# Fusion block on one core: q and k rows regrouped by one transfer of 128 partitions, weight columns in dimension-major order

## The chip, the core and the metric

The kernel runs on one core of a Trainium2 chip. Its engines are TensorE (PE, matmuls; PEld is its loading of weights), VectorE (DVE), ScalarE (ACT), GpSimd (POOL) and SyncE (SP). SyncE computes nothing here; it issues DMA transfers from a queue, in the order of the program. The metric is the time of the whole program on the device, in microseconds (us), as the median of several runs. Lower is better.

## What is computed

The reference makes a sequence `h` of 128 rows out of a state-space kernel and 77 rows of text, for each of 32 images (205 rows of 1024 numbers), and sends it through attention and a linear layer:

```python
h = _L0_tok_ref(log_dt, Lambda, x, 1024)
h = jnp.concatenate([h, txt], axis=1)                       # (32, 205, 1024)
h = h + attn(_layernorm(h), wq, wk, wv, wo)
h = h + ffn(_layernorm(h), W_base, b_base, enc0, enc1, ...)

# attn: NH = 32 query heads, NKV = 8 key and value heads, HD = 32
q = (x @ wq).reshape(b, s, NH, HD)
k = (x @ wk).reshape(b, s, NKV, HD)
v = (x @ wv).reshape(b, s, NKV, HD)
k, v = jnp.repeat(k, 4, axis=2), jnp.repeat(v, 4, axis=2)
scores = jnp.einsum('bihd,bjhd->bhij', q, k) * HD ** -0.5   # causal mask
out = jnp.einsum('bhij,bjhd->bihd', softmax(scores), v)
return out.reshape(b, s, NH * HD) @ wo
```

## The kernel before

The program has three parts, one after the other. `ssm` makes the 128 rows of each image and ends near 185 us. `attention` is a software pipeline over the 32 images, which are called blocks. `tail` multiplies by `wo` and runs the linear layer, from about 1797 us to the end.

In `attention` each engine runs the same `step(b)` for b from -4 to 32. In a step, TensorE works on several blocks at once. It projects block b+2: units `q` 0 to 7, `k` 0 and 1, `v` 0 and 1, each of 24 matmuls. It takes the scores of block b+1 a first time, for their maxima (`score_rows`, L1000 to L1007). And it takes the transposed scores of block b (`scores`, L956 and L959), whose exponentials ScalarE and GpSimd turn into weights for `weigh` (L986). In the first steps only some of that exists: step -2 projects block 0, step -1 projects block 1 and takes the maxima of block 0, step 0 is the first with everything.

All numbers are carried as a high and a low half-precision part. A `q` unit gives 128 columns of the projection, which are four heads of 32 dimensions, so that `qsh` and `qsl` hold in partition 32r + d the dimension d of head 4n + r. The scores want something else: `qst` holds for each head 96 partitions, high, high and low part of its 32 dimensions (`kst`: high, low, high), so that one matmul makes all three products, and two rows more, 96 and 97, with the maxima (`mh`, `ml`). Bringing q and k from the one layout into the other is `restack` (L572). Since it changes partitions, it is done by DMA: for each of the three parts and each r of four, 32 partitions are copied to 32 others. A k unit holds four of the eight key heads, which are moved in the same way. Blocks take turns in two buffers, `qst0`/`qst1` and `kst0`/`kst1`.

SyncE's order in a step is:

1. K1, Q1: the restacks of the second half of the heads of block b+1, whose last unit was projected at the end of the step before;
2. `shift_rows(1)`: two rows of maxima for block b (heads 16 to 31), L617 and L618;
3. in step -1 alone: the loads `ahead` (L597), `wo` with 4 MB and 14 smaller ones, that the tail wants;
4. the four transposes of block b+3 (L623, L624), twice a high and a low part, which TensorE projects in the next step. ScalarE may only overwrite the source `xfh` when they have landed (`high_part`, L717);
5. K0, Q0: the restacks of the first half of block b+2;
6. `shift_rows(0)`: the rows of maxima for heads 0 to 15 of block b+1.

K0 or K1 waits for the low part of its `k` unit and until the scores of an older block no longer need the buffer (`st_filled`); Q0 waits for `q` unit 3 and Q1 for `q` unit 7 (`pj_lo`, counted up by VectorE at L868). TensorE waits for Q and K at L990 and L991 in front of L1000, and for the rows of maxima in front of L956.

Of the kernel before, what the change touches and what calls it, by code (L numbers as in the profile page):

```python
# [8 lines left out]
F16 = mybir.dt.float16  # L9
BF16 = mybir.dt.bfloat16  # L10
I32 = mybir.dt.int32
ALU = mybir.AluOpType
# [4 lines left out]
P = 128  # L17
# [4 lines left out]
D = 1024  # L22
TXT = 77
S = H + TXT
# [397 lines left out]
def attention(nc, ahead, hcat, acat, st, qkv, arena, all_peaks, peaks_in, ksc, spare):  # L422
# [7 lines left out]
    with ExitStack() as ctx:  # L430
# [13 lines left out]
        qsh, qsl = sb("qsh", [P, KC, S], F16), sb("qsl", [P, KC, S], F16)  # L444
        ksh, ksl = sb("ksh", [P, 2, S], F16), sb("ksl", [P, 2, S], F16)
        mh, ml = sb("mh", [NH // 2, 2, S], F16), sb("ml", [NH // 2, 2, S], F16)
        qst = [sb(f"qst{i}", [STACK + 2, NH, S], F16) for i in range(2)]
        kst = [sb(f"kst{i}", [STACK + 2, NKV, S], F16) for i in range(2)]
        vh = [sb(f"vh{i}", [P, 2, NKV, HD + 1], F16) for i in range(3)]
        vl = [sb(f"vl{i}", [P, 2, NKV, HD + 1], F16) for i in range(3)]  # L450
# [1 line left out]
        p32 = arena[:, 0:12 * S].rearrange("p (a k x) -> p a k x", a=2, k=3)  # L452
        ph = sb("ph", [P, 2, 3, 2 * S], F16)
        pl = sb("pl", [P, 2, 3, 2 * S], F16)
        mx = sb("mx", [P, 2, NH])
        seen = sb("seen", [P, REP, P], BF16)
        rden = sb("rden", [P, 2, REP])
        ao = arena[:, 12 * S:12 * S + 2 * D].rearrange("p (h t x) -> p h t x", h=2, t=2)
# [93 lines left out]
        def free_place(eng, kind, n, b):  # L552

            if kind == "q":
                wait(eng, q_in[n // 4], 16 * 12 * (b + 2))
            if kind == "k":
                wait(eng, k_in[n], 16 * 12 * (b + 2))
            if kind == "v":
                wait(eng, av_done, 8 * b)
            if kind == "m":  # L560
                wait(eng, m_in[n], 32 * (b + 1 - n))
# [3 lines left out]
        @block.sync  # L565
        def _(sp):
            def restack(parts_, dst, cs, arrived):

                for k, src in enumerate(parts_):
                    rows = dst[k * HD:(k + 1) * HD].rearrange("d (c r) i -> d c r i", r=4)  # L570
                    for r in range(4):
                        sp.dma_start(rows[:, cs, r, :], src[r * HD:(r + 1) * HD, cs, :]).then_inc(arrived, 16)  # L572

            Q_PARTS, K_PARTS = (qsh, qsh, qsl), (ksh, ksl, ksh)
            HALVES = (slice(0, KC // 2), slice(KC // 2, KC))

            def step(b, par, has):
                base = before(b, par)
                rows = units(has)
                nxt = 1 - par  # L580
                if has["max"]:

                    wait(sp, st_filled, 24 * b)
                    prev = parts(b - 1)
                    wait(sp, pj_lo, before(b - 1, nxt) + at(units(prev), "k", 1) + 1)
                    restack(K_PARTS, kst[nxt], slice(1, 2), k_in[1])
                    wait(sp, pj_lo, before(b - 1, nxt) + at(units(prev), "q", NKV - 1) + 1)
                    restack(Q_PARTS, qst[nxt], HALVES[1], q_in[1])
                if has["att"]:

                    wait(sp, pj_lo, base + at(rows, "m", 1) + 1)
                    shift_rows(1, par)
                if b == -1:

                    sp.wait_ge(w_lo, 2 * KC)
                    for dst, src, arrived in ahead:
                        sp.dma_start(dst, src).then_inc(arrived, 16)  # L597
                if has["turn"]:

                    wait(sp, pj_filled, base)  # L600
                    turn(0, nxt, b + 3)
                    turn(1, nxt, b + 3)
                if has["qkv"]:

                    wait(sp, pj_lo, base + at(rows, "k", 0) + 1)
                    wait(sp, st_filled, 24 * b + 12)
                    restack(K_PARTS, kst[par], slice(0, 1), k_in[0])
                    wait(sp, pj_lo, base + at(rows, "q", 3) + 1)
                    restack(Q_PARTS, qst[par], HALVES[0], q_in[0])
                if has["max"]:  # L610

                    wait(sp, pj_lo, base + at(rows, "m", 0) + 1)
                    shift_rows(0, nxt)

            def shift_rows(half, to):
                heads = slice(half * (NH // 2), (half + 1) * (NH // 2))
                sp.dma_start(qst[to][STACK:STACK + 1, heads, :], mh[:, half, :]).then_inc(m_in[half], 16)  # L617
                sp.dma_start(qst[to][STACK + 1:STACK + 2, heads, :], ml[:, half, :]).then_inc(m_in[half], 16)  # L618

            def turn(t, to, n):  # L620
                r, cols = ((P, slice(0, P)), (TROWS, slice(P, P + TROWS)))[t]
                sp.wait_ge(x_lo, 4 * n + 2 * t + 2)
                sp.dma_start_transpose(out=xth[:, to, :, cols], in_=xfh[0:r, t, :]).then_inc(xt_in[t], 16)  # L623
                sp.dma_start_transpose(out=xtl[:, to, :, cols], in_=xfl[0:r, t, :]).then_inc(xt_in[t], 16)  # L624

            steps(sp, step)
            for q in a_out:
                sp.wait_ge(q, 32 * B)
# [152 lines left out]
        def _(dve):  # L781
# [58 lines left out]
            def take_maxes(b, j, base, ks, late_read):  # L840
                for k in ks:
                    dve.wait_ge(s_filled, 24 * (b + 1) + 3 * j + k + 1)
                    if j == 0 and k == 0:

                        wait(dve, pj_filled, base)
                    if j == NKV // 2 and k == 0 and late_read:

                        dve.wait_ge(pj_filled, base + late_read)
                    src = psS[(j + k) % 2]
                    if k == 0:  # L850
                        if j == 0:
                            dve.wait_ge(mask_ok, 1)
                        for r in range(REP):
                            m = dve.tensor_tensor_reduce(seen[:, r, :], src[:, r * P:(r + 1) * P], mask[:, 0, :], 1.0, LEAST,  # L854
                                                         ALU.add, ALU.max, mx[:, 0, 4 * j + r:4 * j + r + 1])
                        m.then_inc(s_read, 1)
                    else:
                        v = src[0:TXT, 0:2 * S].rearrange("p (h i) -> p h i", i=S)
                        dst = mx[0:TXT, 1, 4 * j + 2 * k - 2:4 * j + 2 * k]
                        dve.tensor_reduce(dst, v, AX.X, ALU.max).then_inc(s_read, 1)  # L860

            def split_unit(b, par, bank, kind, m, count_):
# [81 lines left out]
        def _(pe):  # L944
            pe.wait_ge(const_ok, 1)

            def scores(b, par, g, k):

                if g % 4 == 0 and k == 0:

                    pe.wait_ge(m_in[g // 4], 32 * (b + 1))
                K, Q = kst[par], qst[par]
                wait(pe, exp_done, 24 * b + 3 * g + k - 1)
                ps = psT[(g + k) % 2]
                if k < 2:
                    m = pe.matmul(ps[:, 0:2 * S], K[:, g, 0:P], Q[:, 4 * g + 2 * k:4 * g + 2 * k + 2, :],  # L956
                                  start=True, stop=True)
                else:
                    m = pe.matmul(ps[0:TXT, 0:REP * TXT], K[:, g, P:S], Q[:, 4 * g:4 * g + 4, P:S],  # L959
                                  start=True, stop=True)  # L960
                m.then_inc(st_filled, 1)

# [27 lines left out]
            def score_rows(b, par, j, k):  # L990


                pe.wait_ge(q_in[j // 4], 16 * 12 * (b + 1))
                pe.wait_ge(k_in[j // 4], 16 * 12 * (b + 1))
                K, Q = kst[par], qst[par]
                wait(pe, s_read, 24 * b + 3 * j + k - 1)
                ps = psS[(j + k) % 2]
                if k == 0:
                    for r in range(REP):
                        m = pe.matmul(ps[:, r * P:(r + 1) * P], Q[0:STACK, 4 * j + r, 0:P], K[0:STACK, j, 0:P],  # L1000
                                      start=True, stop=True)
                else:
                    v = ps[0:TXT, 0:2 * S].rearrange("p (h i) -> p h i", i=S)
                    pe.matmul(v[:, :, P:S], ident_bf[0:TXT, 0:TXT], mask[0:TXT, 0:2, 0:TXT],
                              start=True, stop=False, skip_group_check=True)
                    for r in range(2):
                        m = pe.matmul(v[:, r, :], Q[0:STACK, 4 * j + 2 * (k - 1) + r, P:S], K[0:STACK, j, :],  # L1007
                                      start=False, stop=r == 1, skip_group_check=True)
                m.then_inc(s_filled, 1)

            def unit(kind, n, bank, b, par, ks):
# [16 lines left out]
                elif not last:  # L1028
                    return
                elif kind == "m":  # L1030

                    heads = slice(n * (NH // 2), (n + 1) * (NH // 2))
                    pe.wait_ge(s_read, 24 * (b + 1) + 12 * (1 - n))
                    pe.transpose(ps[0:NH // 2, 0:P], mx[:, 0, heads], ident[:])
                    m = pe.transpose(ps[0:NH // 2, P:S], mx[0:TXT, 1, heads], ident[0:TXT, 0:TXT])
                if last:
                    m.then_inc(pj_filled, 1)

# [439 lines left out]
```

## Time and profile before

| | us |
|---|---|
| median of 3 runs | 2941.69 |
| lowest and highest | 2940.85, 2944.85 |
| the profiled execution | 2947.19 |
| its span, first to last instruction | 2945.1 |
| TensorE busy | 2695.8 |
| VectorE busy | 1940.4 |
| ScalarE busy | 1201.6 |
| GpSimd busy | 1144.2 |

The mean granted clock of TensorE in the profiled execution was 0.969 of full. All times of the trace count from the start of the span. In a list of waits a row is "who at which line <- whom it waited for", with total, number and longest. In a timeline, "SPq L572 ... x4" are four issues by SyncE's queue, with the time from the start of the first to the end of the last; a value in brackets at the end is how long the engine had been idle, and for whom. The releaser is the one that the profile shows as the last. Windows sum the busy time of each engine within a stretch; a granted clock of 0.50 is 1.2 GHz and one of 1.00 is 2.4 GHz.

### The profile page before, as it was taken

To read this page: it belongs to the slowest core of one execution; us is meant where nothing else is said; L and a number is where in the kernel's file an instruction comes from. 1 tells how busy PE (TensorE), PEld (TensorE's weight loads), DVE (VectorE), ACT (ScalarE), POOL (GpSimd) and SP (SyncE) were. 2 spreads that over 40 slices of the span, in tenths; PEclk is the share of its full clock that TensorE was granted. 3 is DMA by queue.
4 is the path that set the end of the run, shared out by engine and by line. 5 is a ranking of instruction groups with operands and counts; after the bars stand their busy time and mean duration, and the time that the engine had idled before them with its cause. 6 is when DMAs were issued, how large, how long until landed. Compare 5 with 4: busy or idle time off the path is not lost. (4 is left out here: it accounts for less than half of the span.)

```text
span 2945.1 us, 70977 instructions
## 1 busy us (share of the span) xinstructions
PE 2695.8 (92%) x27456; PEld 1949.7 (66%) x27456; DVE 1940.4 (66%) x5569; ACT 1201.6 (41%) x2506; POOL 1144.2 (39%) x1811
## 2 busy tenths in 40 slices
PE   1948699999999999999999986999999999999999
PEld 1837589989898998989899972444444444444444
DVE  8964488887888888788888774744444444444443
ACT  4342466676766767666666663101010100101010
POOL 2751266565656656566565563101111010101110
PEclk9978899999999999999999995899999999999999
DMA  7754534434343443435344325354554555454543
GB/s 240 190 123 112 87 88 96 98 77 98 82 102 85 93 98 77 99 82 103 81 95 87 66 55 178 79 139 115 136 123 128 131 119 134 119 140 115 136 122 81
DMA packets 564334, 324.72 MB, mean 110 GB/s; under 512 B 501016, under 2 KB 519704, under 8 KB 563520
## 3 DMA queue, kind: packets, MB, share of 16 engines
q1 hardware_dynamic: 541488, 256.35, 39.2%
q10 hardware_dynamic: 22512, 63.84, 6.9%
q8 instruction: 219, 3.59, 0.5%
q14 instruction: 115, 0.94, 0.1%
HBM read 116.49 MB, written 80.61 MB: 67 GB/s over the span
## 5 line engine op out<-in xcount | busy, mean ns | idle before, releaser
L1018 PE MATMUL psJ<-xth,qh 128*128 128x205 f16 x2048 | 520.3, 254 | 52.4 <-DMA xtl<-xfl 46.9
L689 POOL TENSOR_TENSOR pl<-arena,ph 128x410 f16<-128x410 f32 (+1 forms) x512 | 499.5, 995 | 94.7 <-ACT ph L765 94.7
L1020 PE MATMUL psJ<-xth,ql 128*128 128x205 f16 x2048 | 519.0, 253 | 0.0
L1019 PE MATMUL psJ<-xtl,qh 128*128 128x205 f16 x2048 | 518.6, 253 | 0.0
L684 POOL TENSOR_SCALAR_AFFINE_SELECT arena<-arena 128x256 f32<-128x256 f32 (+1 forms) x768 | 331.6, 438 | 475.5 <-ACT arena L758 454.5
L1243 POOL TENSOR_TENSOR arena<-stage,arena 128x1024 f32<-128x1024 f32 x52 | 122.2, 2349 | 938.1 <-DVE stage L1286 938.1
L1257 ACT CAST xh<-arena 128x1024 f16<-128x1024 f32 x52 | 54.3, 1045 | 998.3 <-DVE arena L1295 998.3
L758 ACT ACTIVATE arena<-psT,escale 128x410 f32<-128x410 f32 (+1 forms) x768 | 401.1, 567 | 119.0 <-PE psT L959 59.7
L765 ACT CAST ph<-arena 128x410 f16<-128x410 f32 (+1 forms) x768 | 334.8, 500 | 15.8 <-POOL arena L684 15.5
L1286 DVE SCALAR_TENSOR_TENSOR stage<-ps5O,osc,h_in 128x512 f32<-128x512 f32 x104 | 78.0, 751 | 390.6 <-PE ps5O L1383 390.6
L860 DVE TENSOR_REDUCE mx<-psS 77x2 f32<-77x410 f32 x512 | 295.4, 577 | 39.8 <-PE psS L1007 32.3
L1381 PE MATMUL ps5F<-wfh,xth 128*128 128x512 f16 x832 | 315.4, 379 | 3.1 <-DMA xtl<-xl 2.0
L1382 PE MATMUL ps5O<-wol,ath 128*128 128x512 f16 x832 | 316.3, 380 | 0.0
L1381 PE MATMUL ps5O<-woh,ath 128*128 128x512 f16 x832 | 316.3, 380 | 0.0
L1383 PE MATMUL ps5O<-woh,atl 128*128 128x512 f16 x832 | 316.2, 380 | 0.0
L854 DVE CUSTOM_DVE_ANT_0 seen<-psS,mask 128x128 bf16<-128x128 f32 x1024 | 235.3, 286 | 121.5 <-PE psS L1000 121.5
L1382 PE MATMUL ps5F<-wfl,xth 128*128 128x512 f16 x832 | 315.3, 379 | 0.0
L1383 PE MATMUL ps5F<-wfh,xtl 128*128 128x512 f16 x832 | 315.3, 379 | 0.0
L986 PE MATMUL psO<-vh,ph 128*128 128x33 f16 (+1 forms) x3072 | 261.2, 178 | 5.1 <-issue 4.7
L986 PE MATMUL psO<-vl,ph 128*128 128x33 f16 (+1 forms) x3072 | 260.4, 178 | 0.0
L986 PE MATMUL psO<-vh,pl 128*128 128x33 f16 (+1 forms) x3072 | 260.4, 178 | 0.0
L986 PEld LDWEIGHTS psO<-vh,ph 128*128 128x128 f16 (+1 forms) x3072 | 245.2, 97 | 7.3 <-issue 6.3
(234 smaller groups left out, 6143.7 us busy)
## 6 DMA issues: line engine op xcount, KB each, us to landing
a_in<-acat SPq DMA_DIRECT2D x52, 512.0 KB, 3.8
h_in<-hcat SPq DMA_DIRECT2D x52, 512.0 KB, 4.6
qst<-qsh SPq DMA_DIRECT2D x512, 51.2 KB, 2.1
out<-stage SPq DMA_DIRECT2D x51, 512.0 KB, 3.1
hcat<-ob SPq DMA_DIRECT2D x64, 256.0 KB, 4.5
xin<-hcat ACTq DMA_DIRECT2D x32, 512.0 KB
acat<-arena ACTq DMA_DIRECT2D x64, 256.0 KB
qst<-qsl SPq DMA_DIRECT2D x256, 51.2 KB, 2.5
```

The lines of the kernel that those rows point to most:

```text
L684: pool.affine_select(out=v, in_=v, compare_op=ALU.is_ge, fill=0.0, base=0, pattern=[[0, v.shape[1]], [1, w]], channel_multiplier=-1).then_ ...
L689: pool.tensor_tensor(view(pl, g % 2, k), view(p32, g % 2, k), view(ph, g % 2, k), ALU.subtract).then_inc(lo_pool, 1)
L758: act.activation(view(p32, g % 2, k), ps_view(psT[(g + k) % 2], k), ACT.Exp, scale=(escale[:, 0:1] if k < 2 else escale[0:TXT, 0:1])).then ...
L765: act.copy(view(ph, g % 2, k), view(p32, g % 2, k)).then_inc(hi_done, 1)
L860: dve.tensor_reduce(dst, v, AX.X, ALU.max).then_inc(s_read, 1)
L986: m = pe.matmul(o[:, t, r, :], p, v[0:T[j], j, g, :], start=n == 0, stop=n == len(list_) - 1)
L1018: pe.matmul(ps[:, 0:S], wh[:, k, c], xth[:, par, k, 0:S], start=k == 0, stop=False)
L1019: pe.matmul(ps[:, 0:S], wh[:, k, c], xtl[:, par, k, 0:S], start=False, stop=False)
L1020: m = pe.matmul(ps[:, 0:S], wl[:, k, c], xth[:, par, k, 0:S], start=False, stop=k == KC - 1)
L1381: pe.matmul(ps[h][:], th[:, k, :], wh[:, k, c], start=k == 0, stop=False)
L1382: pe.matmul(ps[h][:], th[:, k, :], wl[:, k, c], start=False, stop=False)
L1383: m = pe.matmul(ps[h][:], tl[:, k, :], wh[:, k, c], start=False, stop=k == KC - 1)
```

## The change

The columns of `wq` and `wk` are put in another order before they go to the device: within each group of 128, dimension first and head second, where it was head first. So `qsh` now holds in partition 4d + r the dimension d of head 4n + r. Read in order of partitions, that is the order (d, r), and the destination `qst` is laid out to match: its heads are stored by half, r and chunk, `[STACK + 2, 2, REP, NKV // 2, S]` instead of `[STACK + 2, NH, S]`. One transfer then reads 128 partitions with 4 x 205 neighbouring numbers each (1640 bytes) and writes 32 partitions with four such runs. For k it is 128 partitions with 205 numbers each. A restack has 3 issues instead of 12, and the semaphores are counted in 16 x 3 instead of 16 x 12. `mx`, the maxima, is stored in the same order as `qst`, and the matmuls address q and the maxima accordingly: L956 takes its two heads from two places 820 numbers apart, where they were neighbours. Products, sums and their number are the same.

```diff
-        qst = [sb(f"qst{i}", [STACK + 2, NH, S], F16) for i in range(2)]
+        qst = [sb(f"qst{i}", [STACK + 2, 2, REP, NKV // 2, S], F16) for i in range(2)]
-        mx = sb("mx", [P, 2, NH])
+        mx = sb("mx", [P, 2, 2, REP, NKV // 2])
...
-                wait(eng, q_in[n // 4], 16 * 12 * (b + 2))
+                wait(eng, q_in[n // 4], 16 * 3 * (b + 2))
...
                 for k, src in enumerate(parts_):
-                    rows = dst[k * HD:(k + 1) * HD].rearrange("d (c r) i -> d c r i", r=4)
-                    for r in range(4):
-                        sp.dma_start(rows[:, cs, r, :], src[r * HD:(r + 1) * HD, cs, :]).then_inc(arrived, 16)
+                    sp.dma_start(dst[k * HD:(k + 1) * HD], src[:, cs, :]).then_inc(arrived, 16)
...
-                    restack(Q_PARTS, qst[nxt], HALVES[1], q_in[1])
+                    restack(Q_PARTS, qst[nxt][:, 1], HALVES[1], q_in[1])
...
-                sp.dma_start(qst[to][STACK:STACK + 1, heads, :], mh[:, half, :]).then_inc(m_in[half], 16)
+                sp.dma_start(qst[to][STACK:STACK + 1, half], mh[:, half, :]).then_inc(m_in[half], 16)
...
-                        dst = mx[0:TXT, 1, 4 * j + 2 * k - 2:4 * j + 2 * k]
+                        dst = mx[0:TXT, 1, j // 4, 2 * k - 2:2 * k, j % 4]
...
-                    m = pe.matmul(ps[:, 0:2 * S], K[:, g, 0:P], Q[:, 4 * g + 2 * k:4 * g + 2 * k + 2, :],
+                    m = pe.matmul(ps[:, 0:2 * S], K[:, g, 0:P], Q[:, g // 4, 2 * k:2 * k + 2, g % 4, :],
...
+        if name in ("L0_attn_wq", "L0_attn_wk"):
+            a = a.reshape(D, -1, 4, HD).transpose(0, 1, 3, 2).reshape(D, -1)
```

The order of the instructions on TensorE, VectorE, ScalarE and GpSimd is as before. SyncE's queue is shorter in two places that matter below. The first is in step -1, K1 and Q1 of block 0 and behind them the first of the loads `ahead`. Before:

```order
L572 DMA kst0<-ksh 32x205 x4
L572 DMA kst0<-ksl 32x205 x4
L572 DMA kst0<-ksh 32x205 x4
L572 DMA qst0<-qsh 32x4x205 x8
L572 DMA qst0<-qsl 32x4x205 x4
L597 DMA stage<-in_L0_attn_wo 128x8x1024
```

Now:

```order
L573 DMA kst0<-ksh 32x4x205
L573 DMA kst0<-ksl 32x4x205
L573 DMA kst0<-ksh 32x4x205
L573 DMA qst0<-qsh 32x4x820 x2
L573 DMA qst0<-qsl 32x4x820
L598 DMA stage<-in_L0_attn_wo 128x8x1024
```

24 issues stand in front of the load of `wo` before, six now. In a row of the queue the numbers behind the names are the shape of the destination.

The second place is later in the same step, between the last two transposes of block 2 and the rows of maxima of block 0 (`mh`, `ml`), with K0 and Q0 of block 1 between them. Before:

```order
L624 DMA_TRANSPOSE xtl<-xfl 128x8x80
L572 DMA kst1<-ksh 32x205 x4
L572 DMA kst1<-ksl 32x205 x4
L572 DMA kst1<-ksh 32x205 x4
L572 DMA qst1<-qsh 32x4x205 x8
L572 DMA qst1<-qsl 32x4x205 x4
L617 DMA qst0<-mh 1x16x205
L618 DMA qst0<-ml 1x16x205
```

Now:

```order
L624 DMA_TRANSPOSE xtl<-xfl 128x8x80
L573 DMA kst1<-ksh 32x4x205
L573 DMA kst1<-ksl 32x4x205
L573 DMA kst1<-ksh 32x4x205
L573 DMA qst1<-qsh 32x4x820 x2
L573 DMA qst1<-qsl 32x4x820
L617 DMA qst0<-mh 1x16x205
L618 DMA qst0<-ml 1x16x205
```

Here too 24 issues between the transposes and `mh` have become six. The same pattern stands twice in each later step.

## Rows read from the trace of the kernel before

**Rows 1.** Windows: busy us (x instructions) by engine, granted clock, DMA share, GB/s.

```profile
800.00:1000.00 200.00, 192.49 (x2923) 179.68 (x2924) 163.05 (x553) 129.45 (x294) 119.48 (x220) 1.00 0.42 89
```

**Rows 2.** Waits of TensorE, 600 to 1600 us: total us, times, longest us.

```profile
PE psS L1004 <- DVE mx L854: 30.9, 44, 1.1
```

**Rows 3.** Waits of SyncE's DMA queue, 600 to 1600 us.

```profile
SPq L572 <- PE psT L959: 37.2, 22, 2.7
```

**Rows 4.** Waits of TensorE over the whole span.

```profile
PE psJ L1018 <- DMA xtl<-xfl: 46.9, 1, 46.9
...
PE psS L1000 <- DMA qst<-qsl: 5.9, 1, 5.9
```

**Rows 5.** Timeline of ScalarE and TensorE: start us, us, work, [idle before <-releaser].

```profile
310.62 0.72 ACT L717 ACTIVATE xin<-xin,nmean 128x512 f32<-128x512 f32 x1 [17.17 <-DMA xtl<-xfl]
...
313.35 0.32 PE L1004 MATMUL psS<-mask,ident_bf 77*77 77x154 bf16 x1 [14.03 <-DVE mx L860]
...
329.69 0.86 PE L956 MATMUL psT<-qst,kst 98*128 98x410 f16 x2 [12.09 <-DMA qst<-ml]
```

**Rows 6.** Timeline of SyncE's queue, 247 to 330 us: start us, us, issues.

```profile
248.33 2.52 SPq L572 DMA_DIRECT2D kst<-ksh  x4
...
280.74 0.59 SPq L597 DMA_DIRECT2D stage<-in_L_attn_wo  x1
...
282.88 11.87 SPq L597 DMA_DIRECT2D mk<-in_L_ffn_mask  x1
...
305.80 1.28 SPq L623 DMA_TRANSPOSE xth<-xfh  x1
...
311.16 2.49 SPq L572 DMA_DIRECT2D kst<-ksh  x4
...
327.74 0.59 SPq L618 DMA_DIRECT2D qst<-ml  x1
```

**Rows 7.** Tile qst, 600 to 1600 us: duration ns min/median/max, then us to landing.

```profile
L956 PE MATMUL psT<-qst,kst x341: 333/337/340, 599.8 to 1593.1; 98*128 98x410 f16 x171
L572 SPq DMA_DIRECT2D qst<-qsh x340: 585/602/1832, 599.7 to 1600.0; - x170
...
L959 PE MATMUL psT<-qst,kst x171: 298/299/328, 602.5 to 1594.8; 98*77 98x308 f16 x171
...
DMA to landing us min/median/max: 1.9/2.1/4.0
```

**Rows 8.** Timeline of VectorE, 255 to 300 us.

```profile
260.64 0.37 DVE L868 TENSOR_TENSOR qsl<-psJ,qsh 128x205 f16<-128x205 f32 x1
...
294.89 0.35 DVE L866 SCALAR_TENSOR_TENSOR ml<-psJ,mh 16x205 f16<-16x205 f32 x1
```

**Rows 9.** Windows, as in rows 1, in the order of time.

```profile
266.00:272.00 6.00, 5.87 (x36) 5.25 (x37) 2.66 (x11) 0.15 (x1) 0.00 (x0) 0.50 0.10 23
285.00:299.00 14.00, 13.82 (x165) 13.55 (x163) 9.13 (x47) 1.55 (x5) 2.53 (x13) 1.00 1.05 327
330.00:333.00 3.00, 3.00 (x20) 2.56 (x19) 1.42 (x9) 2.38 (x3) 0.65 (x2) 0.50 0.09 22
...
1748.00:1753.00 5.00, 4.61 (x58) 3.52 (x57) 3.13 (x13) 3.68 (x9) 3.26 (x5) 0.50 0.02 5
```

**Rows 10.** Timelines of SyncE's queue, VectorE and TensorE, 1727 to 1748 us.

```profile
1727.78 2.43 SPq L572 DMA_DIRECT2D kst<-ksh  x4
...
1745.58 0.59 SPq L618 DMA_DIRECT2D qst<-ml  x1
...
1735.43 0.35 DVE L866 SCALAR_TENSOR_TENSOR ml<-psJ,mh 16x205 f16<-16x205 f32 x1
...
1747.54 0.86 PE L956 MATMUL psT<-qst,kst 98*128 98x410 f16 x2 [4.74 <-DMA qst<-ml]
```

**Rows 11.** Timelines of SyncE's queue and TensorE, a step in the middle.

```profile
1024.97 0.59 SPq L618 DMA_DIRECT2D qst<-ml  x1
...
1030.03 0.51 PE L956 MATMUL psT<-qst,kst 98*128 98x410 f16 x2
```

More of the change, by code:

```diff
@@ L554, in free_place @@
             if kind == "q":
-                wait(eng, q_in[n // 4], 16 * 12 * (b + 2))
+                wait(eng, q_in[n // 4], 16 * 3 * (b + 2))
             if kind == "k":
-                wait(eng, k_in[n], 16 * 12 * (b + 2))
+                wait(eng, k_in[n], 16 * 3 * (b + 2))
             if kind == "v":
@@ L585, in step @@
                     wait(sp, pj_lo, before(b - 1, nxt) + at(units(prev), "k", 1) + 1)
-                    restack(K_PARTS, kst[nxt], slice(1, 2), k_in[1])
+                    restack(K_PARTS, kst[nxt][:, 4:8], slice(1, 2), k_in[1])
                     wait(sp, pj_lo, before(b - 1, nxt) + at(units(prev), "q", NKV - 1) + 1)
-                    restack(Q_PARTS, qst[nxt], HALVES[1], q_in[1])
+                    restack(Q_PARTS, qst[nxt][:, 1], HALVES[1], q_in[1])
                 if has["att"]:
@@ L606, in step @@
                     wait(sp, st_filled, 24 * b + 12)
-                    restack(K_PARTS, kst[par], slice(0, 1), k_in[0])
+                    restack(K_PARTS, kst[par][:, 0:4], slice(0, 1), k_in[0])
                     wait(sp, pj_lo, base + at(rows, "q", 3) + 1)
-                    restack(Q_PARTS, qst[par], HALVES[0], q_in[0])
+                    restack(Q_PARTS, qst[par][:, 0], HALVES[0], q_in[0])
                 if has["max"]:
@@ L615, in shift_rows @@
             def shift_rows(half, to):
-                heads = slice(half * (NH // 2), (half + 1) * (NH // 2))
-                sp.dma_start(qst[to][STACK:STACK + 1, heads, :], mh[:, half, :]).then_inc(m_in[half], 16)
-                sp.dma_start(qst[to][STACK + 1:STACK + 2, heads, :], ml[:, half, :]).then_inc(m_in[half], 16)
+                sp.dma_start(qst[to][STACK:STACK + 1, half], mh[:, half, :]).then_inc(m_in[half], 16)
+                sp.dma_start(qst[to][STACK + 1:STACK + 2, half], ml[:, half, :]).then_inc(m_in[half], 16)
             def turn(t, to, n):
@@ L854, in take_maxes @@
                             m = dve.tensor_tensor_reduce(seen[:, r, :], src[:, r * P:(r + 1) * P], mask[:, 0, :], 1.0, LEAST,
-                                                         ALU.add, ALU.max, mx[:, 0, 4 * j + r:4 * j + r + 1])
+                                                         ALU.add, ALU.max, mx[:, 0, j // 4, r, j % 4:j % 4 + 1])
                         m.then_inc(s_read, 1)
@@ L955, in scores @@
                 if k < 2:
-                    m = pe.matmul(ps[:, 0:2 * S], K[:, g, 0:P], Q[:, 4 * g + 2 * k:4 * g + 2 * k + 2, :],
+                    m = pe.matmul(ps[:, 0:2 * S], K[:, g, 0:P], Q[:, g // 4, 2 * k:2 * k + 2, g % 4, :],
                                   start=True, stop=True)
                 else:
-                    m = pe.matmul(ps[0:TXT, 0:REP * TXT], K[:, g, P:S], Q[:, 4 * g:4 * g + 4, P:S],
+                    m = pe.matmul(ps[0:TXT, 0:REP * TXT], K[:, g, P:S], Q[:, g // 4, :, g % 4, P:S],
                                   start=True, stop=True)
@@ L990, in score_rows @@
             def score_rows(b, par, j, k):
-                pe.wait_ge(q_in[j // 4], 16 * 12 * (b + 1))
-                pe.wait_ge(k_in[j // 4], 16 * 12 * (b + 1))
+                pe.wait_ge(q_in[j // 4], 16 * 3 * (b + 1))
+                pe.wait_ge(k_in[j // 4], 16 * 3 * (b + 1))
                 K, Q = kst[par], qst[par]
@@ L999, in score_rows @@
                     for r in range(REP):
-                        m = pe.matmul(ps[:, r * P:(r + 1) * P], Q[0:STACK, 4 * j + r, 0:P], K[0:STACK, j, 0:P],
+                        m = pe.matmul(ps[:, r * P:(r + 1) * P], Q[0:STACK, j // 4, r, j % 4, 0:P], K[0:STACK, j, 0:P],
                                       start=True, stop=True)
@@ L1006, in score_rows @@
                     for r in range(2):
-                        m = pe.matmul(v[:, r, :], Q[0:STACK, 4 * j + 2 * (k - 1) + r, P:S], K[0:STACK, j, :],
+                        m = pe.matmul(v[:, r, :], Q[0:STACK, j // 4, 2 * (k - 1) + r, j % 4, P:S], K[0:STACK, j, :],
                                       start=False, stop=r == 1, skip_group_check=True)
@@ L1030, in unit @@
                 elif kind == "m":
-                    heads = slice(n * (NH // 2), (n + 1) * (NH // 2))
                     pe.wait_ge(s_read, 24 * (b + 1) + 12 * (1 - n))
-                    pe.transpose(ps[0:NH // 2, 0:P], mx[:, 0, heads], ident[:])
-                    m = pe.transpose(ps[0:NH // 2, P:S], mx[0:TXT, 1, heads], ident[0:TXT, 0:TXT])
+                    pe.transpose(ps[0:NH // 2, 0:P], mx[:, 0, n].rearrange("p r c -> p (r c)"), ident[:])
+                    m = pe.transpose(ps[0:NH // 2, P:S], mx[0:TXT, 1, n].rearrange("p r c -> p (r c)"), ident[0:TXT, 0:TXT])
                 if last:
```

## The prediction

> **What bounds the kernel now.** First the stages. In 800 to 1000 us, the middle of the attention part (about 225 to 1795 us), TensorE is busy 192.5 of 200 us at full clock, with the DMA engines at a share of 0.42 [rows 1]. The list of who waited for whom, for 600 to 1600 us, tells what the gaps are: TensorE's largest wait is for VectorE's maxima, 30.9 us in 44 pieces, and no wait for a DMA is in its list [rows 2]. SyncE's queue, which issues every transfer that the change touches, waits there for TensorE: 22 times at the restack line, 37.2 us [rows 3]. In the steady state the queue is ahead of the work, and a shorter queue gives nothing.
>
> The same list over the whole span shows where TensorE does wait for DMAs [rows 4]. The 46.9 us at L1018 come in front of the first projection, before there is anything to restack; they stay. The 5.9 us at L1000 are for q rows. Two more stand in the order of time: at L956, 12.09 us until 329.69 for an ml row, and at L1004, 14.03 us until 313.35, put down to VectorE [rows 5]. That one is a DMA in disguise: ScalarE sits for 17.17 us until 310.62, for the transposes of block 2, and its casts, VectorE and TensorE come behind it. Why are those transposes late? SyncE's queue in order of time answers: restacks from 248.33 on, at 280.74 the first of 15 loads of later weights, among them a stall (11.87 us), and only at 305.80 the transposes [rows 6]. The start of the attention part is bound by the issuing queue, its middle by TensorE.
>
> **What one transfer costs.** A restack takes 12 issues for k and 12 for q. Four k issues of 12.8 KB took 2.52 us [rows 6], one q issue of 51.2 KB 0.60 in the median, landing 2.1 us after it [rows 7]; 24 of them and one mh row fill the time from 311.16 to 327.74, so 0.66 us apiece with gaps [rows 6]. After the change it is 3 and 3, each with 128 runs, where a q transfer had 128 already (4 chunks on 32 partitions) and a k transfer 32. The load of 4 MB took 0.59 us to issue [rows 6]. So the price hardly follows size. I take 0.66; the bounds are 0.59 and, from the scatter of q issues, 1.83. 32 blocks save 36 issues each, 1152 in all, some 760 us of the queue, nearly all of it hidden.
>
> On this the Trainium skill ("DMA: Bandwidth & Descriptors", section "Issuing engines are not separate DMA queues") says that the time the sequencer needs to start a DMA is usually small relative to the DMA itself. Here the trace disagrees: 12 issues take 7.9 us, and the last lands 2.1 us later. By the rule the whole sum below would be near zero.
>
> **Term A, the transposes of block 2.** VectorE ends the low part of q unit 7 at 261.01, the last data that block 0's restacks need [rows 8]. The nine issues before it then need only 5.9 us from 248.33 and are out of the way. Q1 goes at 261.0 and ends at 263.0, so the weight loads start at 263.0 instead of 280.74, 17.7 us sooner; no wait holds them. Their 25 us, stall included, go along, as the stall looks like a ring full behind 4 MB; I subtract 0.7 us because 614 KB of q now lie right in front of them. A = 17. Can the compute chain follow? It loses the 5.9 us wait (Q0 lands near 255, wanted at 260.2) and the slow clock behind it (266 to 272 us at 0.50 [rows 9], 3 us). ScalarE reaches its wait about 8.9 us sooner than 293.45, near 284.6; the transposes land at 293.6. They are still last, by 9 us, and the 5.9 us are inside A, not beside it. TensorE resumes at 296.3 after an idle of some 6 us instead of 14; the clock probably falls all the same, so the shorter idle gives 0.5 us.
>
> **Term B, the row of maxima of block 0.** TensorE waits 12.09 us for the ml row issued at 327.74, behind 24 restack issues from 311.16 on [rows 5, 6]. The row itself was made by 295.2 [rows 8]. Six issues take 4.0 us instead of 15.9: 11.9 less, and TensorE comes to it as long after resuming as now, so the row and TensorE meet within 1 us. B = 12. Behind this wait the clock stood at 0.50 (330 to 333 [rows 9]), some 3.8 us that do 1.9 us of work; I take 1.5.
>
> **Term C, the last restack.** At 1742.8 us TensorE starts to wait 4.74 us for block 30's ml row, issued at 1745.58 behind 24 issues from 1727.78 on [rows 10]. That step projects nothing, is short, and the slack is gone. ml is ready at 1735.78, and q unit 7 before it on VectorE; even if Q1 had to wait until then, it and the row would land by 1741. Nobody waits for that: 4.7 us. Behind the wait 1748 to 1753 ran at 0.50 [rows 9], but ScalarE and GpSimd share the bound there: 1.5 of 3 us.
>
> **Steady state, and what the change adds.** One ml row per block is close: issued at 1024.97, landed near 1027.0, wanted at 1030.03 [rows 11]; that slack only grows. The moving operand of L956 becomes two runs of 205 columns, that of L959 stays four. L956 takes 337 ns for 410 columns, L959 299 for 308 in runs [rows 7]; 102 columns are 42.5 ns at 2.4 GHz, the difference is 38, so the cuts cost 4.5 ns at most. On 512 instructions that is 0 to 2.3 us; I take 0, as matmuls issue pipelined. Maxima are written with a stride, two elements each: 0. The host's column order is outside the timed program. Q packets fall from 98,304 to 24,576, which could shorten other landings; nothing waits for them: 0.
>
> **Sum.** 17 + 0.5 + 12 + 1.5 + 4.7 + 1.5 = 37.2 us. The span 2945.1 becomes 2907.9. The profiled execution took 2947.19 (the span and 2.1 around it), 5.5 above the median 2941.69; the saving, a difference, is taken from the median: 2904.5, say **2905 us**.
>
> **Rivals.**
> (1) The weight loads do not move as a block. In 285 to 299 us the DMA engines are at 1.05 [rows 9], so their drain and not the issue could set the end; if the stall grows by what the queue saves, A and its 0.5 go, and B and C stay: 19.7, **2922 us**. Against it: in 266 to 272 the engines stood at 0.10 [rows 9], room to start early. 13%.
> (2) An issue of 128 partitions costs 1.24 us. A is then 15, B 8.5, C whole: 31.7, **2910 us**, inside the forecast's own range. 12%.
> (3) The change does not do for the queue what it says: the price of an issue follows its partitions, about 2.6 us each, and three take as long as twelve. A, B and C vanish: **2942 us**. Against it: the 128-partition load at 0.59 [rows 6]. 6%.
> (4) Slower. Source and destination now differ in shape (128 partitions against 32 with four runs), and the transfer is spread over fewer DMA engines. Place: every restack, with transposes and ml rows behind it. Restack bytes are 24 x (51.2 + 12.8) KB, 1.57 MB a block; 89 GB/s at a share of 0.42 [rows 1] make 212 GB/s on 16 engines. A block lasts 46.9 us (341 L956 in 1000 us, 16 a block [rows 7]), other traffic takes 12.3 of it, so it decides below 45 GB/s, 3.4 engines. On two it is 59 + 12 = 71 us a block, 25 more in each of 32: **near 3700 us**. No row speaks for it. 4%.
> The Trainium skill (same page, section "Why a DMA increments its semaphore by 16 and not by 1") takes the number of engines, up to 16, from the slowest dimensions of both sides; 128 and 32 both divide by 16, so by it rival 4 does not occur. No row here shows a transfer with unlike sides.
>
> **How the numbers follow.** The forecast with A, B and C: 65%, 2895 to 2915. Its low end is a shorter stretch of loads, up to the 9 us at which the compute chain is last; its high end small shortfalls in each term. With rivals 1 and 2 the range is **2895 to 2924**. About 0.2% (5.9 us) is what a measurement of this kernel can tell from no change. Faster 0.90, same 0.06, slower 0.04.
>
> **What would show it.** Right: restack issues at 0.6 to 0.7 us, the wo load issued near 263, the first block-2 transpose near 288, ScalarE's 17.2 us wait at about 9, TensorE's two waits for ml gone, a steady block as long as before. Wrong: wo near 263 but the transposes still near 305 (rival 1); issues above 1 us (2, 3); TensorE waiting for qst or transposes between 600 and 1600 us (4).

## The result and the profile after

The changed kernel takes 2904.99 us in the median of 4 runs (2903.69 to 2910.03), against 2943.27 us before: a ratio of 0.9873 (95% interval 0.9856 to 0.9890), 1.3% faster. 2905 us had been forecast, from a median before of 2941.69. Its profiled execution took 2910.03 us with a span of 2907.9, 37.2 us less than the span before.

First, TensorE's waits over the whole span (engine and line <- whom it waited for: us in total, times, longest):

```profile
PE psJ L1018 <- DMA xtl<-xfl: 47.9, 1, 47.9
PE psS L1004 <- DVE mx L854: 42.8, 63, 1.1
...
PE psS L1004 <- DVE mx L860: 7.0, 1, 7.0
...
PE psT L956 <- DMA qst<-ml: 2.2, 1, 2.2
```

The wait at L1018 in front of the first projection stayed, as did the steady one for VectorE's maxima. The 5.9 us of [rows 4] for q rows are gone from the list. The waits that ended at 313.35 and 329.69 us [rows 5], 14.03 and 12.09 us, are now 7.0 and 2.2, and the 4.74 us of [rows 10] are gone.

SyncE's queue in order of time, to be read beside [rows 6], and with it the three ends of waits of [rows 5]:

```profile
258.11 1.19 SPq L573 DMA_DIRECT2D qst<-qsh  x2
...
260.00 0.60 SPq L598 DMA_DIRECT2D stage<-in_L_attn_wo  x1
...
262.44 9.76 SPq L598 DMA_DIRECT2D mk<-in_L_ffn_mask  x1
...
287.29 1.27 SPq L623 DMA_TRANSPOSE xth<-xfh  x1
...
292.65 0.59 SPq L573 DMA_DIRECT2D kst<-ksh  x1
...
297.17 0.59 SPq L618 DMA_DIRECT2D qst<-ml  x1
```

```profile
292.14 0.72 ACT L717 ACTIVATE xin<-xin,nmean 128x512 f32<-128x512 f32 x1 [10.13 <-DMA xtl<-xfl]
...
294.87 0.32 PE L1004 MATMUL psS<-mask,ident_bf 77*77 77x154 bf16 x1 [6.99 <-DVE mx L860]
...
302.30 0.52 PE L956 MATMUL psT<-qst,kst 98*128 98x410 f16 x2 [2.22 <-DMA qst<-ml]
```

The load of `wo` goes out at 260.00 instead of 280.74, the first transpose of block 2 at 287.29 instead of 305.80, and the stall on a mask load is still there with 9.76 us. ScalarE goes on at 292.14 instead of 310.62. The ml row is issued at 297.17, but TensorE gets it only at 302.30.

Where the 37.2 us arise can be read from the same event in both traces. The table gives how much earlier each comes in the changed kernel.

| event | before, us | after, us | earlier by | added |
|---|---|---|---|---|
| first projection (L1018) | 224.91 | 224.56 | 0.35 | 0.35 |
| low part of q unit 7, block 0 | 260.64 | 257.71 | 2.93 | 2.6 |
| ScalarE resumes (L717) | 310.62 | 292.14 | 18.48 | 15.55 |
| first scores of block 0 (L956) | 329.69 | 302.30 | 27.39 | 8.9 |
| store of block 29's second half | 1736.22 | 1704.84 | 31.38 | 4.0 |
| last store of attention | 1793.6 | 1756.2 | 37.4 | 6.0 |
| end of the span | 2945.1 | 2907.9 | 37.2 | -0.2 |

The change can have no part in the first two rows: the first projection lies ahead of all restacks, and the 2.9 us of the second row were there when the first restack was issued, at 248.33 us before and 245.39 after.

### The profile page after: what moved, and what is told of

Read it like the earlier page. It is cut to its first block and busy times, and to the rows that moved or that the text cites. A ratio compares the mean times of both kernels' runs of the same rounds, so it can differ in the third digit from the quotient of the medians.

```text
span 2907.9 us, 69825 instructions
## 1 busy us (share of the span) xinstructions
PE 2689.5 (92%) x27456; PEld 1946.0 (67%) x27456; DVE 1941.5 (67%) x5569; ACT 1201.6 (41%) x2506; POOL 1142.4 (39%) x1811
## 3 DMA queue, kind: packets, MB, share of 16 engines
q1 hardware_dynamic: 449328, 256.28, 41.7%
## 5 line engine op out<-in xcount | busy, mean ns | idle before, releaser
L1018 PE MATMUL psJ<-xth,qh 128*128 128x205 f16 x2048 | 519.5, 254 | 51.4 <-DMA xtl<-xfl 47.9
```

Of the source, the lines that this page charges most:

```text
L1018: pe.matmul(ps[:, 0:S], wh[:, k, c], xth[:, par, k, 0:S], start=k == 0, stop=False)
```

## Experiments

### Twelve issues in the new layout

The issue count was undone and everything else kept, in two ways. In the first, q moves chunk by chunk: the source has 128 partitions still, and the runs are 410 bytes as before the change.

```diff
-                    sp.dma_start(dst[k * HD:(k + 1) * HD], src[:, cs, :]).then_inc(arrived, 16)
+                    for r in range(4):
+                        if cs.stop - cs.start == 4:
+                            sp.dma_start(dst[k * HD:(k + 1) * HD, :, r], src[:, cs.start + r, :]).then_inc(arrived, 16)
+                        else:
+                            sp.dma_start(dst[k * HD + 8 * r:k * HD + 8 * r + 8], src[r * HD:(r + 1) * HD, cs, :]).then_inc(arrived, 16)
```

> The layout of the changed kernel, but 12 issues per restack again: q moved chunk by chunk (410-byte runs, 128 source partitions to 32), k in four quarters of its source partitions (32 to 8). If the number of issues on SyncE's queue is the cause, all of the gain goes: 2942 us, within 6, with the load of wo issued near 280, the first transpose of block 2 near 305, and TensorE's waits for ml back at about 12 and 4.7 us. If the layout of q, the column order or the 128-partition source were the cause, it stays near 2905.

It took 2945.2 us, ratio to the kernel before 1.0006 (0.9996 to 1.0015). In the second, both q and k are cut by partitions (the last line of the diff for both), so that q keeps its runs of 1640 bytes:

> The changed kernel with each of its transfers cut into four by source partitions (32 to 8), so 12 issues again, but with runs of 1640 bytes for q as in the changed kernel. Issue count as the cause: 2942 to 2946 us, like the cut by chunks (2945.2). Longer runs as the cause: 2905 to 2912.

2947.34 us, ratio 1.0017 (1.0008 to 1.0026). TensorE's waits in the two, first by chunks over the whole span, then by partitions from 225 to 345 us (L1004 and L1001 are the line of L1000, L960 and L957 that of L956, L1008 and L1005 that of L1004):

```profile
PE psT L960 <- DMA qst<-ml: 18.6, 3, 12.1
...
PE psS L1008 <- DVE mx L864: 15.8, 1, 15.8
...
PE psS L1004 <- DMA qst<-qsl: 6.7, 1, 6.7
```

```profile
PE psS L1005 <- DVE mx L861: 14.2, 1, 14.2
PE psT L957 <- DMA qst<-ml: 13.4, 1, 13.4
PE psS L1001 <- DMA qst<-qsl: 8.3, 1, 8.3
```

All the old waits are back, with the layout, the column order and, in the second, the run length of the changed kernel. All of the gain is the number of issues. The layout by itself gives nothing; cut by partitions, it is 0.17% slower than before, and a q issue held the queue for 0.67 us in the median instead of 0.60.

### Which blocks carry it

With a condition in front of the same loop, only some blocks were cut again, and the semaphores were counted accordingly:

```diff
+                    if SPLIT(n):
+                        for r in range(4):
...
+                    else:
+                        sp.dma_start(dst[k * HD:(k + 1) * HD], src[:, cs, :]).then_inc(arrived, 16)
```

Blocks 2 to 29 cut (`2 <= n < B - 2`):

> Three issues per restack for blocks 0, 1, 30 and 31, twelve for the 28 blocks between. If only the start and the end count, it is as fast as the changed kernel: 2905 us, within 4. If the changed kernel also gains in the steady state (its stores of block outputs come 27.5 us sooner at block 0 and 31.4 at block 29, so 3.9 us in between), up to 2909. If the gain came from fewer packets or issues all along, 28 of 32 blocks of it would be lost: near 2938.

2909.02 us, ratio 0.9875 (0.9859 to 0.9892). These four runs (2905.49 to 2913.47) overlap those of the changed kernel (2903.69 to 2910.03), so the 4.0 us between the medians are not shown by the times alone; the traces, further down, bear them out.

Blocks 0 and 1 cut (`n < 2`):

> Twelve issues for blocks 0 and 1, three for all others. Terms A and B go, term C and what the middle gives stay. In the two profiles A was 15.5 us, B 8.9, C 6.3: 2905 + 24 to 27 = 2929 to 2932 us. If the middle were the cause it would stay near 2908.

2930.94 us, ratio 0.9956 (0.9941 to 0.9970), with the waits of the start as before the change (L1021 and L1017 are L1004 and L1000):

```profile
PE psS L1021 <- DVE mx L877: 15.5, 1, 15.5
...
PE psT L973 <- DMA qst<-ml: 12.2, 1, 12.2
PE psS L1017 <- DMA qst<-qsl: 6.9, 1, 6.9
```

Blocks 30 and 31 cut (`n >= B - 2`):

> Twelve issues for blocks 30 and 31 alone, three for the others. Term C goes: 4.7 us of waiting and about 1.5 of clock, 2905 + 6 = 2911 us, with TensorE waiting for the ml row of block 30 once more, 3 to 5 us. If C was nothing but a shift of waits, 2905.

2915.91 us, ratio 0.9901 (0.9886 to 0.9916).

Against 2905.0, twelve issues cost 4.0 us in 28 blocks of the middle, 25.9 in the first two and 10.9 in the last two. The sum, 40.8, is close to the 40.2 that they cost everywhere (2945.2 - 2905.0). So the start and the end carry nine tenths, four blocks of 32.

The end costs more than the 6 us expected. TensorE's wait is back in the timeline, and what follows it ran at the low clock (the last line is the window 1715 to 1725 us, with the granted clock third from the end):

```profile
1714.88 0.87 PE L973 MATMUL psT<-qst,kst 98*128 98x410 f16 x2 [4.83 <-DMA qst<-ml]
...
1715.00:1725.00 10.00, 9.23 (x110) 6.76 (x109) 7.14 (x32) 6.96 (x15) 7.11 (x11) 0.50 0.14 47
```

The same window of the changed kernel, at a similar point of its work:

```profile
1715.00:1725.00 10.00, 7.58 (x148) 5.64 (x146) 9.62 (x42) 8.97 (x21) 9.00 (x16) 1.00 0.14 46
```

With the wait, the clock is 0.50 from 1712 us to the end of attention; without it, 1.00 until 1726, and it falls there too, after TensorE had been busy 7.6 of 10 us. Before the change it fell behind the wait as well, but came back to 1.00 from 1753 to 1763.

What that costs can be read from the time between the store of block 29's second half and the last store of attention. With twelve issues at the end it was 57.4 us in the kernel before, where the clock came back, and 58.9 to 59.9 us in this run and three others, where it did not; with three issues it was 50.6 to 51.4 us in five runs. So this run lost 7.6 us there against the changed kernel, 4.8 of them the wait, and the rest goes with the clock. The other 3 us of the 10.9 are not in this part of the trace and stay unexplained; the two profiled spans differ by only 6.1 us.

### The later loads, moved out of the way

The waiting transposes stand behind the 15 loads of `ahead`. These were taken out of step -1 and issued one by one, each behind the transposes of a step from 2 to 16:

```diff
                 if b == -1:
                     sp.wait_ge(w_lo, 2 * KC)
-                    for dst, src, arrived in ahead:
-                        sp.dma_start(dst, src).then_inc(arrived, 16)
...
                     turn(1, nxt, b + 3)
+                if 2 <= b < 2 + len(ahead):
+                    dst, src, arrived = ahead[b - 2]
+                    sp.dma_start(dst, src).then_inc(arrived, 16)
```

In the kernel before:

> The kernel before, with the 15 later loads taken out of step -1 and issued one per step behind the transposes of steps 2 to 16. The transposes of block 2 then go out near 281 instead of 306 us, ScalarE's wait of 17 us and TensorE's 14.0 vanish; the 24 issues of K0 and Q0 now run from about 287 to 303, and TensorE waits some 4 us for the ml row instead of 12.1. Sum 24: 2918 us, within 5. If the late transposes were only a symptom, it stays at 2942.

2918.97 us, ratio 0.9916 (0.9899 to 0.9932). SyncE's queue (first transpose, K0, ml) and the end of TensorE's wait (L957 is L956):

```profile
278.19 1.25 SPq L624 DMA_TRANSPOSE xth<-xfh  x1
...
284.36 2.49 SPq L572 DMA_DIRECT2D kst<-ksh  x4
...
301.16 0.59 SPq L619 DMA_DIRECT2D qst<-ml  x1
...
303.08 0.86 PE L957 MATMUL psT<-qst,kst 98*128 98x410 f16 x2 [4.06 <-DMA qst<-ml]
```

The order was as expected, a transpose at 278.19, and 24 issues in front of ml: the wait of 12.1 us is 4.06. So the transposes and the ml row are two separate waits behind one queue.

In the changed kernel:

> The same move of the loads in the changed kernel. Its ScalarE wait of 10.1 us and TensorE's 7.0 and 2.2 us vanish, with some 2 to 3 us of slow clock behind them: 2893 us, within 3. If the 15 loads collide with the steady steps and cost there what they give at the start, 2900 to 2905.

2894.45 us, ratio 0.9834 (0.9817 to 0.9851), 10.5 us below the changed kernel. It is faster than either kernel. Its queue, and all of TensorE's waits over 1 us between 225 and 345 us:

```profile
260.40 1.44 SPq L624 DMA_TRANSPOSE xth<-xfh  x1
...
284.78 0.59 SPq L619 DMA_DIRECT2D qst<-ml  x1
...
PE psJ L1019 <- DVE qsl L869: 3.0, 2, 2.8
PE psT L960 <- ACT arena L759: 2.0, 2, 1.8
PE psS L1005 <- DVE mx L855: 1.6, 3, 1.1
```

The transposes go out right behind Q1, at 260.40, and the ml row when its data is made, at 284.78. No wait for a DMA is left in this stretch. The loads, one at a time, took 0.58 to 0.90 us to issue, and none stalled.

### The ml row in front of q

> The changed kernel with mh and ml of block 0 issued in front of K0 and Q0 of block 1 in step -1. In the changed kernel ml was issued at 297.17 and TensorE waited until 302.30, 2.2 us, with the DMA engines near full. If the row is late because 614 KB of q were queued in front of it, it now lands within about 2.5 us and that wait goes, though the q rows land 1.3 us later and may be waited for instead: 2903 to 2905 us. If the row's 5 us have another cause, the wait is 1 us at least, as before.

```diff
+                if b == -1:
+                    wait(sp, pj_lo, base + at(rows, "m", 0) + 1)
+                    shift_rows(0, nxt)
                 if has["qkv"]:
...
-                if has["max"]:
+                if has["max"] and b > -1:
```

2906.85 us, ratio 0.9880 (0.9865 to 0.9895): no gain over 2905.0. The queue (ml, then the last q issue) and TensorE (L1003 is L1000):

```profile
291.13 0.59 SPq L621 DMA_DIRECT2D qst<-ml  x1
...
295.02 0.62 SPq L573 DMA_DIRECT2D qst<-qsl  x1
...
300.77 0.61 PE L1003 MATMUL psS<-kst,qst 96*128 96x128 f16 x4 [2.83 <-DMA qst<-qsl]
```

The wait for ml has gone and one of 2.83 us for the q rows has come. Those were issued at 295.02 and waited for until 300.77, 5.7 us later, which is no delay of that moment: 5.6 us is their median over the whole changed kernel. Putting the row first only changes who is last, as the restack's own data takes that long.

## Why the prediction was right, and where it was not

The total was right and the cause was right, but three of its terms were off: A by 1.5 us and B by 4.6 too high, the middle by 4 too low.

**Term A** was 17 and 0.5 for the clock, and measured 15.5. Its mechanism held point by point: Q1 as soon as its data was there, `wo` right behind it, the stretch of loads moving along. But that stretch, from `wo` to the first transpose, grew from 25.06 to 27.29 us, where 0.7 had been allowed. ScalarE's wait was to be 9 us and was 10.13. That the stall in it is a full ring is a guess that no run tested. Rival 1, that the stretch would grow by all the queue saved, is out: it grew by 2.2 of 17.7.

**Term B** was 12 and 1.5 for the clock, and measured 8.9. The step that failed is "the row and TensorE meet within 1 us". The issue was on time, 9.9 us behind the first transpose, where it had been 21.9. But the landing was taken as 2.0 us from the rows before, and it took 5.1. That is the 3.1 us between the 12 and the 8.9. In the changed kernel the window of these transfers reads (DMA share and GB/s at the end):

```profile
294.00:302.00 8.00, 5.22 (x30) 4.40 (x30) 5.27 (x17) 4.39 (x8) 0.00 (x0) 0.63 0.88 118
```

0.88 of the engines' time for 118 GB/s. The same 614 KB of q rows are now asked for within 1.9 us where it took 7.7 (319.31 to 327.05), and the page gives what one transfer takes to land, before and now (the last number, us in the median):

```profile
qst<-qsl SPq DMA_DIRECT2D x256, 51.2 KB, 2.5
```

```profile
qst<-qsl SPq DMA_DIRECT2D x64, 205.0 KB, 5.6
```

The last q transfer in front of the row was issued at 295.86 us, so by that median it lands near 301.5, and TensorE had the row at 302.30. Between 600 and 1600 us, where no q transfer stands right in front of them, ml rows landed in 1.9 us in the median. That the row waits for the packets ahead of it is a reading of these numbers; the last experiment fits it, since there the row, issued first, was not waited for.

The clock gave nothing here: TensorE took 5.21 us for the work between its two waits (294.87 to 300.08, granted clock 0.52), where the same 30 matmuls had taken 4.25 us (313.35 to 317.60, at 0.64), and behind the second wait it fell to 0.50 again. So the 0.5 us of term A and the 1.5 of term B did not come.

**Term C** was 4.7 and 1.5, and measured 6.0 in the trace (the expectations above say 6.3). Undone alone it cost 10.9 in the medians, of which the clock, which did not come back there, explains a part.

**The middle** was put at 0 and gave 4.0. "In the steady state the queue is ahead of the work, and a shorter queue gives nothing" was wrong. The row of [rows 3] is the largest of a list that adds up to only 74 of the 1000 us from 600 to 1600: for 93% of the time the queue was at its issues, and it just kept up. In the changed kernel its waits there add up to 635 us, and the largest is now for data that is not made yet:

```profile
SPq L617 <- DVE ml L866: 250.6, 43, 6.7
```

The list of TensorE's waits had no DMA in it, true; but ScalarE issues DMAs as well, the stores of each block's output. One place from the kernel before, ScalarE's queue, SyncE's queue and TensorE:

```profile
1161.32 2.01 ACTq L706 DMA_DIRECT2D acat<-arena  x1
...
1160.85 3.77 SPq L572 DMA_DIRECT2D qst<-qsl  x4
...
1164.09 0.33 PE L959 MATMUL psT<-qst,kst 98*77 98x308 f16 x1 [1.67 <-ACT arena L758]
```

One issue of ScalarE took 2.01 us while SyncE was issuing (four of its own took 3.77 us instead of 2.53), and TensorE waited 1.67 us for ScalarE's exponentials. The same store in the changed kernel:

```profile
1132.78 0.40 ACTq L706 DMA_DIRECT2D acat<-arena  x1
```

From 400 to 1700 us ScalarE's 160 to 162 issues took 72.0 us before, and 69.8, 71.4, 70.8 and 72.8 us in the other kernels with twelve issues in the middle; with three they took 66.5, 64.8, 65.8, 65.8 and 67.8. From block 0's first store to block 29's last took 1367.2 to 1370.7 us in the five kernels with twelve issues and 1362.5 to 1366.6 us in the five with three: they do not overlap, and the means differ by 4.3 us. In the same stretch TensorE waited for ScalarE's exponentials for 12.2 us on average with twelve and 9.1 with three, which is 3.1 of the 4.3. So the size fits. The cause is not isolated: no run took ScalarE's issues away with SyncE's queue unchanged.

**Rivals 2 and 3**, a dearer issue: the q issue took 0.60 us in the median over the span, as before. **Rival 4**, fewer engines and a slower block: no. The transfers did get slower to land, though, and that was the nearest to a loss:

```profile
span 2907.9 us, 69825 instructions
...
q1 hardware_dynamic: 449328, 256.28, 41.7%
...
L956 PE MATMUL psT<-qst,kst x344: 334/335/340, 602.7 to 1599.8; 98*128 98x410 f16 x172
...
L573 SPq DMA_DIRECT2D qst<-qsh x86: 547/572/605, 609.1 to 1591.1; - x86
...
DMA to landing us min/median/max: 1.9/3.8/5.8
```

Landing 3.8 us in the median of the steady stretch where it was 2.1 [rows 7], the small rows of maxima included; q rows alone took 4.7 and 5.6 us (high and low part) where it was 2.1 and 2.5. A transfer is four times as large, though, and a restack as a whole lands sooner: from the first of its three issues to the last landing are some 7 us, where it was some 10 with twelve (estimates: 1.3 and 5.6 us, 7.1 and 2.5). L956 is unchanged within 2 ns, with its operand in two runs.

The packets of SyncE's queue speak to rival 4 as well. Of the 92,160 that have gone, 73,728 are runs of q (98,304 to 24,576); the other 18,432 are 16 for each of the 1,152 issues saved. In the second cut of the first experiment, whose transfers write 8 partitions each, there are 6,144 packets more than in the changed kernel (455,472), which is 8 for each of its 1,536 restack issues against 16 for each of 384. The Trainium skill ("DMA: Bandwidth & Descriptors", section "Why a DMA increments its semaphore by 16 and not by 1") says that each engine which takes part in a DMA issued like these posts one increment of its own; by its rule the outer sizes 128 and 32 give 16 engines, 32 and 8 give 8. The packets agree with both, if the extra ones are these increments, which is inferred. Its remark that issue time is usually small relative to the DMA (section "Issuing engines are not separate DMA queues") does not hold for the kernel before: 0.60 us of issue stood against 2.1 of landing, and twelve in a row were worth 40 us, as the first experiment shows.

Part of the hit was luck. The two spans differ by exactly the 37.2 us of the forecast, but 2.9 of them were there ahead of the first restack; what the change did adds up to 34.5 us in these two traces and 38.3 in the medians. And the 4 us of the middle stand in for the 4.6 that B lacked. The high end of the range, 2924, would have been needed had the stretch of loads grown as in rival 1.

## What to carry to other kernels

A queue that no engine waits for in the steady state can still be the bound for forty microseconds of filling and draining. Add up its own waits, too: here it was free for only 74 of 1000 us, so it had no room to catch up. Look at the first and the last passes of a pipeline in the order of time, and at what an engine's wait stands behind, not at whom it is put down to. Merging transfers pays by the number of issues in front of an urgent one; where one bulky load stands there, moving it gives more (2905 to 2894 us here, and 2941 to 2919 in the kernel before) for three lines. And when you take issues away, ask what comes last next: here it was the landing of the merged transfers, and of a row issued right behind them.

## What the runs showed of the hardware

Fewer and longer packets, moved by fewer and larger transfers, did not relieve the DMA engines. The line of SyncE's queue on the page, before and in the changed kernel above (541,488 and 449,328 packets):

```profile
q1 hardware_dynamic: 541488, 256.35, 39.2%
```

The share of the engines' time rose from 39.2 to 41.7% with 92,160 packets fewer. Cut by partitions into four, with the same long runs, it was 36.2%, and the transfers into `qst` landed in 2.4 us in the median. So it is not the run length that raised it. What did is open: that run has smaller transfers, and each seems to run on 8 engines instead of 16, both at once. Packets of one large transfer may count time in which they wait for one another; no run isolates that.

Behind the 4 MB load, one of the 14 small loads that followed at once held the queue for 10 to 12 us in its issue. Issued one per step, the same loads took under 1 us each. Whether the 4 MB or the number of loads in a row holds it, no run tells apart.

An issue cost the queue about 0.6 us whether it moved 6, 51 or 205 KB. Two queues that issue at the same time seem to delay each other: one issue of ScalarE took 2.01 us instead of 0.40. That is seen together in ten traces and not isolated.
